# Local attention: the position bias goes into PSUM on TensorE, GpSimd's product is dropped, and the inverse norms come from one power on GpSimd

## The reference

```python
attn = jnp.einsum('bhnd,bhmd->bhnm', _l2n(q), _l2n(k)) * scale
rpb = 16.0 * jax.nn.sigmoid(tbl[REL_IDX].reshape(N, N, NH).transpose(2, 0, 1))
attn = attn + rpb[None]
attn = attn.reshape(-1, nW, NH, N, N) + ATTN_MASK[None, :, None]
attn = jax.nn.softmax(attn.reshape(-1, NH, N, N), axis=-1)
out = jnp.einsum('bhnm,bhmd->bhnd', attn, v).transpose(0, 2, 1, 3).reshape(-1, N, C)
```

## Time and profile before

| what | value |
|---|---|
| median of three runs | 3420.02 us (3405.79 to 3424.62) |
| the profiled execution's own time | 3387.51 us |
| its span, first to last instruction | 3385.7 us |
| granted clock over the span | 0.879 |
| attention: first to last exponential (L560) | 99.2 to 966.2 us, 127 steps of 6.83 us |
| granted clock, 110 to 950 us | 0.74 |

### The profile page before, as it was taken

How to read it: one execution, slowest core, us unless ns; L and a number is a source line. 1 busy time by engine, 2 the same in 40 slices (tenths; PEclk the granted TensorE clock), 3 DMA queues, 4 the chain that set the end, 5 groups by cost and what they waited for, 6 DMA issues and landing times. The chain is left out here.

```text
span 3385.7 us, 93300 instructions
## 1 busy us (share of the span) xinstructions
PE 2962.9 (88%) x35559; PEld 2211.9 (65%) x35559; DVE 2441.2 (72%) x6382; ACT 1576.2 (47%) x3047; POOL 1288.1 (38%) x1360
## 2 busy tenths in 40 slices
PE   2899898889979979999888888888882999999999
PEld 1666666666657747777788666666662666666776
DVE  2676767877745558888677678877883677768888
ACT  1555545555524423433200333333330666777887
POOL 0444445555433321111000166666665000017776
PEclk9876767876669979999899989988985999999999
DMA  3000000000012210000000011111112444443333
GB/s 101 17 22 20 23 19 23 23 23 21 18 31 75 73 50 20 26 20 20 2 3 3 24 50 50 51 50 48 50 46 68 85 96 97 97 90 99 99 98 92
DMA packets 293305, 162.69 MB, mean 48 GB/s; under 512 B 93180, under 2 KB 284040, under 8 KB 292616
## 3 DMA queue, kind: packets, MB, share of 16 engines
q1 hardware_dynamic: 276488, 123.14, 13.5%
q0 software_dynamic: 16384, 33.59, 3.3%
HBM read 66.74 MB, written 71.30 MB: 41 GB/s over the span
## 5 line engine op out<-in xcount | busy, mean ns | idle before, releaser
L2302 DVE TENSOR_TENSOR e_glo<-e_g,e_ghi 128x512 f16<-128x512 f32 x540 | 375.1, 695 | 171.7 <-ACT e_ghi L2209 163.5
L2204 ACT ACTIVATE e_g<-psum,b 128x512 f32<-128x512 f32 x540 | 371.1, 687 | 181.7 <-PE psum L2358 164.4
L2188 POOL DMA_INDIRECT e_got<-ys_dram,e_idx x256 | 254.5, 994 | 508.9 <-DMA ys_dram<-e_yo 422.0
L2375 PE MATMUL psum<-w2hi,e_ghi 128*128 (+1 forms) x2160 | 394.7, 219 | 9.2 <-DVE e_glo L2302 7.0
L2379 PE MATMUL psum<-w2hi,e_glo 128*128 (+1 forms) x2160 | 390.1, 219 | 0.0
L2377 PE MATMUL psum<-w2lo,e_ghi 128*128 (+1 forms) x2160 | 390.1, 219 | 0.0
L503 POOL TENSOR_TENSOR pT<-pT,rpbx 128x1024 f32<-128x1024 f32 x128 | 300.7, 2349 | 27.9 <-ACT pT L560 27.9
L1738 POOL DMA_INDIRECT xs_dram<-m_xt,m_idxl x256 | 269.4, 1052 | 105.5 <-issue 72.3
L2375 PEld LDWEIGHTS psum<-w2hi,e_ghi 128*128 128x128 f16 x2160 | 210.8, 98 | 116.4 <-issue 44.9
L698 PE MATMUL psum<-vd,pT 128*64 128x18 f32 x4096 | 183.9, 237 | 62.1 <-ACT mT L565 62.1
L2377 PEld LDWEIGHTS psum<-w2lo,e_ghi 128*128 128x128 f16 x2160 | 211.2, 98 | 38.7 <-issue 0.3
(11 more groups left out here) (331 smaller groups left out, 7731.7 us busy)
## 6 DMA issues: line engine op xcount, KB each, us to landing
ys_dram<-e_yo SPq DMA_DIRECT2D x71, 256.0 KB
f_xm<-x_dram SPq DMA_DIRECT2D x32, 256.0 KB
mid_dram<-f_xm SPq DMA_DIRECT2D x32, 256.0 KB
l_t<-mid_dram SPq DMA_DIRECT2D x16, 512.0 KB
m_t<-mid_dram SPq DMA_DIRECT2D x16, 512.0 KB
res_dram<-m_rest SPq DMA_DIRECT2D x16, 512.0 KB
e_acc<-res_dram SPq DMA_DIRECT2D x32, 256.0 KB
out_dram<-e_acc SPq DMA_DIRECT2D x32, 256.0 KB, 2.2
```

What stands on the lines that cost most here:

```text
L2188: gp.indirect_dma_start(out=got[:, q % 2, k, t, :], out_offset=None, in_=ys, in_offset=bass.IndirectOffsetOnAxis(idx[:, q // 2, i:i + 1], 0))\
L2204: ac.activation(g32[:, c % 4, :], bank(c % 4), ACT.Gelu, bias=bias, scale=1.0 / WSCALE)\
L2302: ve.tensor_tensor(glo[:, c % 4, :], g32[:, c % 4, :], ghi[:, c % 4, :], ALU.subtract)\
L2375: pe.matmul(o, ghi[:, c % 4, g], w2hi[:, e, f, :], start=first and t == 0, stop=False, skip_group_check=True)
```

## The change

The position bias is kept as a half-precision pair (`rpb_hi`, `rpb_lo`) of 16 times the sigmoid, without the exponential. Eight matmuls a pair (`biases`, the identity times the bias, 256 columns each) write it into the PSUM columns of the turned scores before anything else is added there; the exponential of L560 then holds it. POOL's product goes, and `sums` waits for the exponential alone. The seven DVE instructions of the inverse root give way to one POOL instruction, `nrm` to the power -0.5 on 128x64.

```diff
@@ setup, ScalarE
-                            ac.activation(rpbx[half].rearrange("q h n -> q n h"),
-                                          sig[half].rearrange("q n (h k) -> q n h k", k=2)[:, :, :, k], ACT.Exp, scale=16.0)\
+                            ac.activation(rpb_hi[half].rearrange("q h n -> q n h"),
+                                          sig[half].rearrange("q n (h k) -> q n h k", k=2)[:, :, :, k], ACT.Copy, scale=16.0)\
@@ setup, VectorE, after f1lo and before the weights
+                        ve.wait_ge(s_ac, 7)
+                        for k in range(2):
+                            half = slice(64 * k, 64 * k + 64)
+                            ve.scalar_tensor_tensor(out=rpb_lo[half].rearrange("q h n -> q n h"),
+                                                    in0=sig[half].rearrange("q n (h k) -> q n h k", k=2)[:, :, :, k], scalar=16.0,
+                                                    in1=rpb_hi[half].rearrange("q h n -> q n h"), op0=ALU.mult,
+                                                    op1=ALU.subtract).then_inc(s_ve, 1)
@@ attention, GpSimd
-                        if s.real():
-                            met(gp, pr_ok, s)
-                            p = pT[:, s.odd]
-                            e = rpbx[:].rearrange("p (j g) n -> p j (g n)", j=4).unsqueeze(2).to_broadcast([P, 4, 2, 2 * N])
-                            gp.tensor_tensor(p, p, e, ALU.mult).then_inc(pe_ok.sem, 1)
+                        q = s + 4
+                        if not s.odd and q.real():
+                            unit(gp, nm_ok, q)
+                            unit(gp, qn_ok, q - 2)
+                            gp.tensor_tensor(rsq[:, 0, :], nrm[:], nhalf[:, 0:1].to_broadcast([P, 4 * NH]), ALU.pow)\
+                                .then_inc(root_ok.sem, 1)
@@ attention, VectorE
-                        y0, t = rsq[:, 0, :], rsq[:, 1, :]
+                        y0 = rsq[:, 0, :]
                         q = s + 4
                         if not s.odd and q.real():
                             unit(ve, sq_ok, q)
+                            unit(ve, root_ok, q - 2)
                             ve.tensor_reduce(nrm[:], sq[:].rearrange("q (h d) -> q h d", d=HD), X, ALU.add)\
                                 .then_inc(ss_ok.sem, 1)
                             unit(ve, ss_ok, q)
-                            done(q, ve.tensor_scalar(nrm[:], nrm[:], 1e-24, None, ALU.max), 1)
...
+                            ve.tensor_scalar(nrm[:], nrm[:], 1e-24, None, ALU.max).then_inc(nm_ok.sem, 1)
                         q = s + 3
                         if s.odd and q.real():
...
+                            unit(ve, root_ok, q)
                             q3 = qk[:, q.u % 2].rearrange("p a k (h d) -> p (a k h) d", d=HD)
                             ve.tensor_tensor(q3, q3, y0.unsqueeze(2).to_broadcast([P, 4 * NH, HD]), ALU.mult)\
@@ attention, TensorE
+                    def biases(q):
+
+                        met(pe, pr_ok, q - 1)
+                        met(pe, mx_ok, q)
+                        for part in (rpb_hi, rpb_lo):
+                            for j in range(4):
+                                pe.matmul(bank(j)[:, 256:512].rearrange("p (w n) -> p w n", w=2), ident16[:],
+                                          part[:, 2 * j:2 * j + 2, :].rearrange("p g n -> p (g n)").unsqueeze(1)
+                                          .to_broadcast([P, 2, 2 * N]), start=(part is rpb_hi), stop=False, skip_group_check=True)
...
-                        met(pe, pe_ok, q)
+                        met(pe, pr_ok, q)
...
                     def beat(s):
+                        if s.real():
+                            biases(s)
                         if (s + 1).real():
                             scores(s + 1)
```

More of the change, by code:

```diff
@@ L188, in phase_setup @@
                 selk = keep("selk", [P, 4, 4, N], F16)
-                rpbx = keep("rpbx", [P, NH // 2, N])
+                rpb_hi = keep("rpb_hi", [P, NH // 2, N], F16)
+                rpb_lo = keep("rpb_lo", [P, NH // 2, N], F16)
                 vd = keep("vd", [P, 4, 4, NH // 2, 2, HD + 1])
@@ L335, in phase_attention @@
         def phase_attention(c1, W):
-            I32 = mybir.dt.int32
             BF16 = mybir.dt.bfloat16
@@ L340, in sb @@
                 return c1.enter_context(nc.sbuf_tensor(name, shape, dt))
-            wqkT, projT, g1, be1, qb2, pb2, msk, eps, mx2, selk, rpbx, vd = (
-                W[k] for k in "wqkT projT g1 be1 qb2 pb2 msk eps mx2 selk rpbx vd".split())
+            wqkT, projT, g1, be1, qb2, pb2, msk, eps, mx2, selk, rpb_hi, rpb_lo, vd = (
+                W[k] for k in "wqkT projT g1 be1 qb2 pb2 msk eps mx2 selk rpb_hi rpb_lo vd".split())
             xw = sb("xw", [P, NP, C])
@@ L369, in phase_attention @@
             stored = [psig(f"stored{p}", 1, 16) for p in range(NP)]
[L370 removed]
+            (s_ps, mx_ok, mT_ps, mT_ok, t_ps, pr_ok, o_ps, rs_ok, on_ok, onT_ps, onT_ok, v_ps, v_ok, pj_ps, st_ok, mv_ok, h_ok, ve_ok, rstd_ok,
              xb_ok, x1_ok) = (psig(k) for k in (
[L372 removed]
+                 "s_ps mx_ok mT_ps mT_ok t_ps pr_ok o_ps rs_ok on_ok onT_ps onT_ok v_ps v_ok pj_ps st_ok mv_ok h_ok ve_ok rstd_ok "
                  "xb_ok x1_ok").split())
@@ L375, in phase_attention @@
                 psig(k) for k in "xT_ps xT_ok qk_ps qk_ok sq_ok ss_ok qn_ok tr_ps kT_ok".split())
-            qm_ok, newton = psig("qm_ok", 4), psig("newton", 8)
+            qm_ok, nm_ok, root_ok = psig("qm_ok", 4), psig("nm_ok"), psig("root_ok")
             class Pair:
@@ L602, in beat @@
                                                     in1=x1[:, q.p, :], op0=ALU.mult, op1=ALU.add).then_inc(x1_ok.sem, 1)
-                        def done(q, i, n):
-                            i.then_inc(newton.sem, 1)
-                            unit(ve, newton, q, n)
-                        y0, t = rsq[:, 0, :], rsq[:, 1, :]
+                        y0 = rsq[:, 0, :]
                         q = s + 4
@@ L614, in beat @@
                             unit(ve, ss_ok, q)
-                            done(q, ve.tensor_scalar(nrm[:], nrm[:], 1e-24, None, ALU.max), 1)
-                            done(q, ve.tensor_scalar(y0.bitcast(I32), nrm[:].bitcast(I32), -0.5, float(0x5F1FFFF9),
-                                                     ALU.mult, ALU.add), 2)
-                            done(q, ve.tensor_tensor(t, y0, y0, ALU.mult), 3)
-                            done(q, ve.scalar_tensor_tensor(out=t, in0=t, scalar=-1.0, in1=nrm[:], op0=ALU.mult, op1=ALU.mult), 4)
+                            ve.tensor_scalar(nrm[:], nrm[:], 1e-24, None, ALU.max).then_inc(nm_ok.sem, 1)
                         q = s + 3
                         if s.odd and q.real():
-                            done(q, ve.scalar_tensor_tensor(out=y0, in0=t, scalar=C2, in1=y0, op0=ALU.add, op1=ALU.mult), 5)
-                            done(q, ve.tensor_tensor(t, y0, y0, ALU.mult), 6)
-                            done(q, ve.scalar_tensor_tensor(out=t, in0=t, scalar=-0.5 * C1 ** 3 * ONE, in1=nrm[:], op0=ALU.mult,
-                                                            op1=ALU.mult), 7)
-                            done(q, ve.scalar_tensor_tensor(out=y0, in0=t, scalar=1.5 * C1 * ONE, in1=y0, op0=ALU.add,
-                                                            op1=ALU.mult), 8)
+                            unit(ve, root_ok, q)
                             q3 = qk[:, q.u % 2].rearrange("p a k (h d) -> p (a k h) d", d=HD)
@@ L661, in scores @@
                         met(pe, mx_ok, q - 1)
+                        alone = not (q - 1).real()
                         for w in range(2):
@@ L666, in scores @@
                                                   high(qm[rows(j), q.u % 2, q.odd, k, w].rearrange("p g t -> p (g t)")),
-                                                  high(kT[rows(j), q.u % 2, q.odd, half(w)]), start=True, stop=True)
+                                                  high(kT[rows(j), q.u % 2, q.odd, half(w)]), start=alone, stop=True,
+                                                  skip_group_check=True)
                         i.then_inc(s_ps.sem, 1)
@@ L677, in turned_scores @@
                                     pe.matmul(bank(j)[half(k), 256 + P * w:256 + P * w + P], selk[rows(j), q.kind(), 2 * w + k, :],
-                                              mT[rows(j), q.odd, :], start=(w == 0), stop=False, skip_group_check=True)
+                                              mT[rows(j), q.odd, :], start=False, stop=False, skip_group_check=True)
                         for w in range(2):
```

3 lines of the change are left out of this document (removed).

## The result

The changed kernel takes 3710.55 us in the median of four runs (3703.89 to 3723.15), the kernel before 3412.9 us in four (3404.01 to 3424.62). The ratio is 1.087 with a 95% interval of 1.082 to 1.092: slower, by 9%. The forecast was 3702 us in a range of 3630 to 3785. The profiled execution took 3708.24 us, with a span of 3706.4 us.

The account below looks back on a forecast made before the run. PE bounds at half clock, PE and DVE wait for each other at full; the power's ring then sets upper beats. 3387.5 us, +301 for 127 steps, +17 first units, -5 last beats, +1 setup: 3702 us, range 3630 to 3785.

Parts of the forecast that it names:

- The power: Inverse root on POOL, 128x64: 10.4 to 10.8 us by the line through 1, 4 and 8 columns, taken as 10.5.
- The first two rivals: Power under some 5.8 us: about 3520 us (chance 0.06); the same with upper clock held throughout: about 3334 us (0.03).
- The ring: Power to next power through DVE, PE and POOL: 17.5 us for two beats at the upper clock, 18.4 at the lower.
- The lower level: Attention beats at half clock: PE with the bias bounds, 9.95 us a beat, 19.9 for two.
- The bias: Eight added PE matmuls before the rough scores: 0.86 us a beat at the upper clock, 1.71 at the lower.
- The forecast for a cheap power: Attention beat if the power is not last: 6.4 us at full clock, with shorter DVE work giving back PE's waits for maxima.
- The share of the upper clock: Attention phase: upper level 0.6 of the time, against 0.48 before, giving 9.2 us a beat.
- The terms at the ends: Outside the 127 steps: +17 us for two units before the first exponential, +1 setup, -5 for the last four beats.
- The last term: Last four beats have no power and run faster: -5 us.
- L601 and the lock: DVE instruction ahead of L629, held to the power's end by the SBUF rule: some 15 us, left out of the sum.
- The rule of 2.6 cycles an element: Skill page's figure for two-input elementwise instructions on GpSimd: power well under 1 us; set aside for the trace's rows.
- The forecast of the sign: Whole kernel: slower 0.95, faster 0.03, the same 0.02.

Follow-up runs that it names:

- e1: Changed kernel with the inverse root back on DVE in seven small instructions, bias in PSUM and no product kept: 3444.7 us, 1.003 to 1.010 of the kernel before.
- e3: Changed kernel with the power on 32 of the 64 columns, a constant in the rest: 3438.2 us, 1.005 to 1.011 of the kernel before.
- e9: Changed kernel, power kept, with the eight bias matmuls issued one step earlier, ahead of `sums`: 3687.7 us, 1.077 to 1.092 of the kernel before.
- e4: Changed kernel without the bias matmuls, power kept: 3692.0 us, 1.073 to 1.086 of the kernel before.
- e8: Changed kernel with the power on 48 of the 64 columns, a constant in the rest: median 3561.4 us, profiled 3509.96 us, no ratio given.
- e2: Kernel before with only the inverse root replaced by the POOL power; product kept, no bias matmuls: 3850.1 us, 1.119 to 1.134 of the kernel before.
- e5: Kernel before without POOL's product and without bias matmuls, root on DVE, setup as changed: 3406.7 us, 0.995 to 1.004 of the kernel before.

## Why the prediction was right

- **The power.** The line through 1, 4 and 8 columns gave 10.4 to 10.8 us, taken as 10.5; it is 10.54 (L510). The widths of this study (5.44 at 32, 8.02 at 48) lie on it too, within 1.2%. The first two rivals fell with this; e1 and e3 show what a cheap power would have given, 3445 and 3438 us, between their 3520 and 3334.
- **The ring.** 17.5 us at the upper clock and 18.4 at the lower were forecast; the turns are 17.30 (e9) and 18.16 (33 of 60 in the changed kernel, and e4 at 0.50), with the difference in the link from L683 to the projection that was named for it. The links are the ones named: 6.9 us of DVE's wait before L623 in each unit, 2.7 us on PE before L744 in the turn shown. e3 shows the other side, a power that costs nothing once it fits, e8 the ring at 14.78 us with a shorter power, and e9 that an earlier bias does not take it away.
- **The lower level.** 19.9 us for two beats was forecast, set by PE with the bias on it; the turns of e9 that lie wholly at 0.50 take 19.87. The changed kernel has no such turn; its nearest, at 0.60 to 0.62, take 18.88 to 19.20.
- **The bias.** Eight matmuls take 603.75 - 602.77 = 0.98 us at the upper clock and 615.70 - 613.88 = 1.82 at the lower, against 0.86 and 1.71: the streaming that was counted, and 0.1 us more, which I put down to the first weight load; no run shows that. What they add to a beat at the upper clock, with no power, is 6.64 - 5.61 = 1.03 us. The forecast for a cheap power, 6.4 a beat, took that DVE's relief would give back 0.55 us a beat. From before's mean of 5.87 (the pair in the earlier trace rows was a slower one, 6.06) the bias would lead to 6.85, and 6.64 is measured, so 0.2 came back. PE waits for `mT` there (0.37 and 1.11 us in two beats), which comes from ACT; that a freer DVE does not hasten it is argued and not shown.
- **The share of the upper clock** was the weak term. 0.6 was chosen, 0.46 is measured (0.73 over 110 to 1250 us). By the forecast's own formula 0.46 gives 9.36 us a beat and 3722 us. The step was 9.17 against 9.2, and that closeness is partly luck: the sum was made of two kinds of beat, 8.75 and 9.95, of which the changed kernel has hardly any. One turn of 60 is at 17.30 and none at 19.9. Most are the ring with its matmuls at the lower clock (18.16, 9.08 a beat), whatever the clock in the rest of the turn, and the others change level within a turn that PE nearly fills (18.88 to 19.20). The two prices lay on either side of what happened, so their mean held.
- **The terms at the ends.** +16 us up to the first exponential was forecast as 17 for two slow units and 1 for setup. Setup is 7.5 us of it, which leaves 8.5 for the units (in e2, which has the power and not the setup, the first exponential stands at 107.6 against 99.2; against e1, at 110.7, the power adds only 4.5, so the split is rough). Right in the sum, wrong in both parts. The subtractions were priced by L298, which is of contiguous half-precision rows; these write and read with a stride, and take 2.46 us apiece, and ACT's copy before them takes 2.49 against the 1.1 of the exponential it replaced. The last term, -5 us, came out as +7.6 behind the last exponential. From there to the end of the span the twelve kernels of this study take 2419 to 2445 us, with 2427 in the changed one, with and without a power, so this term is not resolved.
- **L601 and the lock.** "SBUF — State Buffer" of the Trainium skill, section "Who interferes with whom", would have L607 held to the power's end. It is not: L607 runs at 598.17 inside a power that lasts from 595.42 to 605.96, and takes 0.34 us; over the whole kernel its longest is 0.352. The product did hold it: the middle duration was 1.10 us in the kernel before and is 1.62 in e2, where product and power are both on POOL, and in e5, with neither, it is 0.343. The rule holds here for POOL's product and not for its power, and leaving its 15 us out was right.
- **The rule of 2.6 cycles an element** from the Trainium skill's "GPSIMD Engine Reference", section "Elementwise — side-by-side cycle accounting", would make the power well under 1 us (an estimate from that page's figure). The measurement is 10.54 us and decides: the page's figure is not for this operation.

The forecast of the sign rested on one thing that could be read before: a dear instruction of 10.5 us, in a place where an in-order engine stands behind it. The clock's part, about which I could argue only in words, had to be small for the numbers to hold, and under the ring it was.

## What to carry to other kernels

Price an instruction at a new width from the same instruction at two others in the trace, and then ask not how busy its engine gets but which ring it stands in: the power was free at 5.4 us and cost 266 us at 10.5. Measure a ring from one start of its own dear instruction to the next: cut at the exponential, the same phase seemed to have beats of 8.7 and 9.9 us, or of 8.0 and 10.6. When an engine's order is in-order and full, look where added work stands before asking what it costs; the same eight matmuls, against the kernel without them (e5), were +0.7% behind `sums` and -1.7% ahead of it. And where TensorE's clock moves, compare beats at one clock first and the share of each second, or a shorter program that is slower can't be understood.

## What the hardware did that I had not expected

- A strided half-precision output is dear on both engines: 64x512 in 2.46 us on DVE and 2.49 on ACT, where ACT's f32 output of the same layout, from the same input, took 1.1 us and DVE's contiguous 128x512 0.69. ACT's two instructions differ in the function as well as in the type, so what part the type and what part the stride has is not separated.
- POOL's power leaves DVE alone (0.34 us for an instruction with two SBUF inputs inside it), while beside POOL's product the same instruction takes 1.10 us in the median and up to 2.1.
- The granted clock rose with work added to PE and with work moved to another place: 0.92 with eight late matmuls, 0.74 with four late ones, 0.70 with none (in the longest of its executions), 1.00 with eight early ones and 0.93 with four early ones. PE was busy 89%, 92%, 93%, 92% and 91% of these stretches, so the busy share, in which matmuls at the lower clock last longer, does not tell them apart.
